# One mixing-and-FFN block of an RWKV-6 layer: the low-rank mix products move from three reduced-precision passes to one float32 product on 32 rows, and the state products move ahead

## The chip, the core and the metric

The kernel runs on one core of a Trainium2 chip. Its engines are TensorE (PE, matrix products; its weight loads are shown apart as PEld), VectorE (DVE), ScalarE (ACT), GpSimd (POOL) and SyncE (SP, which here only issues DMAs). They run side by side and meet at semaphores. The metric is the device time of one launch in microseconds; lower is better.

## The reference

The input x has 4 rows of 1024 tokens with 256 channels. `xn = layernorm(x)`, and the result is x plus two branches of `xn`. Cut to what matters:

```
dxa = shift(xn) - xn;  xm = xn + dxa * miu_x
lora_h = tanh(xm @ A_lora).reshape(b, t, 5, 32)             # five streams of rank 32
miu = lambda_ + einsum('btfi,fic->fbtc', lora_h, B_lora)    # "mix product": [t,32] x [32,256] per stream
w_in, k_in, v_in, r_in, g_in = xn + dxa * miu               # streams W, K, V, R, G
k, v, r = k_in @ Wk.T, v_in @ Wv.T, r_in @ Wr.T;  g = silu(g_in @ Wg.T)
w = td_miu + tanh(w_in @ td_A) @ td_B
y = wkv6(r, k, v, w, u)        # S = diag(exp(-exp(w_t))) S + k_t^T v_t, per head of 64
attn = (groupnorm(y) * g) @ Wo.T
ffn = fp4(silu(fp4(xn) @ fp4(Wgate).T) * (fp4(xn) @ fp4(Wup).T)) @ fp4(Wdown).T   # blocks of 16 quantised
```

## The kernel before

The tokens are worked off in 8 steps of 128 tokens times 4 rows (512 columns, `N`). The 256 channels lie as two halves of 128 partitions. Each step has two parts. `front(step)` makes the shifted input, the LoRA products, the five streams and the projections; beside them it finishes the step before ("tail"): the recurrence, its group norm and output projection, and the FFN units 4 to 7. `levels(step)` runs seven doubling levels of the chunked scan, with FFN units 0 to 3 between them. An FFN "unit" is half of the 704 hidden values of one row: gate and up products on PE (`gate_up`, L313), SiLU on ACT, the product on DVE (`ffn_product`, L875), a block scale (`ffn_scale`, L886: L781 to L787) and rounding (`ffn_round`, L894: L793 to L797) on DVE, the scaling back on POOL (`scale_hidden`, L1148: L1155 and L1158), and per two units the transposes (`hidden_transposes`, L327) and the down product (`down`, L338) on PE. Step 0 has no tail; it quantises the FFN weights there instead (`weight_piece`, L799).

Nothing is planned at run time: each engine has its own instruction list, written out by hand, and works it off in order. A late instruction holds up all behind it on its engine.

The mix products are `mix(f, to)` (L298). The rows of `B_lora` of stream f lie at partitions 32f (stream G at 0) of a tile that is zero elsewhere, so the product contracts 128 rows. For accuracy the tile and the tanh output are each split into a high and a low part in float32r, and three products are summed: 2 halves x 3 = 6 matmuls of 512 columns. The low part of the tanh output costs a copy on ACT (L674) and a subtraction on DVE (`split_hidden`, L861); the weights are split once (ACT L759, DVE L1105). The unsplit weights lie in the buffer `dt`, which POOL clears first (L1255).

Around the change, in `front` with a tail, the orders are:

- PE: recurrence, `down` 0, key transposes (L424), `gate_up` 4, `hidden_transposes` 1, LoRA products (L434), state products (L442), `down` 1, wait for the low part, mix W into pair[0], wait for the state update (L448), mix K into pair[1], `gate_up` 5, decay product (L458), mix V, project K (L464), `hidden_transposes` 2 (it waits for unit 5), decay product 2 (L470), y transposes, `down` 2, `gate_up` 6, mix R, value product (L490), output projection (L394), `gate_up` 7, mix G, project R, transposes, project G.
- DVE: bonus (L949), `shift_mix` (L850), `add_down` 0, `y_stats`, the whole of unit 4, `split_hidden`, the state update (L992, L998), stream W and stream K (L870), `add_down` 1, unit 5, stream V, `head_quant`, and so on.
- POOL: `scale_hidden` 3, `y_centre`, `scale_hidden` 4, add_x W and K (L1146), `y_scale` (L1191), `scale_hidden` 5, add_x V, and so on.

Of the kernel before, what the change touches and what calls it, by code (L numbers as in the profile page):

```python
# [86 lines left out]
def through(step, n=1):  # L87

    return step * n + n


def before(step, n=1):

    return step * n


def later(step):

    return not isinstance(step, int) or step > 0
# [8 lines left out]
def build(nc, x, vecs, w_lora, b_lora, td_a, td_b, w_proj, w_gu, w_dn, ident, masks, head_ones, out):  # L108
    with ExitStack() as ctx:
        def sb(name, shape, dt=F32):  # L110
            return ctx.enter_context(nc.sbuf_tensor(name, shape, dt))
# [7 lines left out]
        walora = sb("walora", [P, HALVES, 2 * P])  # L119
        wblora_hi = sb("wblora_hi", [P, MIXES, C], F32R)  # L120
        wblora_lo = sb("wblora_lo", [P, MIXES, C], F32R)
        wtda = sb("wtda", [P, HALVES, P])
# [23 lines left out]
        xmt = sb("xmt", [P, HALVES, N])  # L146
        lh = xmt
        lh_hi = sb("lh_hi", [P, 2, N], F32R)
        lh_lo = sb("lh_lo", [P, 2, N], F32R)
        xx = sb("xx", [P, MIXES, HALVES, N])  # L150
        tdh = sb("tdh", [P, N])
        ee = sb("ee", [P, HALVES, N])
        dt = sb("dt", [P, 2 * HBS * L])
        wblora = dt[:, 0:MIXES * C].rearrange("p (f c) -> p f c", c=C)
        kk = sb("kk", [P, HBS, L])
# [36 lines left out]
        def sem(name):  # L192
            return ctx.enter_context(nc.semaphore(name))
# [15 lines left out]
        s_bon, s_rup, s_msk, s_y, s_gnvar, s_state = sem("s_bon"), sem("s_rup"), sem("s_msk"), sem("s_y"), sem("s_gnvar"), sem("s_state")  # L209
        s_xql, s_wlo, s_lhi, s_llo, s_bhi, s_blo = sem("s_xql"), sem("s_wlo"), sem("s_lhi"), sem("s_llo"), sem("s_bhi"), sem("s_blo")  # L210
        s_z, s_xqn, s_att, s_hm, s_hqn, s_fo, s_wq = sem("s_z"), sem("s_xqn"), sem("s_att"), sem("s_hm"), sem("s_hqn"), sem("s_fo"), sem("s_wq")
# [22 lines left out]
        def _(sp):  # L234
# [18 lines left out]
            for f in range(4):  # L253
                sp.dma_start(wblora[R_LORA * f:R_LORA * (f + 1), f, :], b_lora[f]).then_inc(s_const, 16)
            sp.dma_start(wblora[0:R_LORA, 4, :], b_lora[4]).then_inc(s_const, 16)
            sp.dma_start(wtda[:, :, 0:TD_R], td_a.rearrange("(h p) c -> p h c", p=P)).then_inc(s_const, 16)
# [18 lines left out]
        def _(pe):  # L275
# [9 lines left out]
            def head_transposes_q(step):  # L285
# [10 lines left out]
                t.then_inc(s_txq, 1)  # L296

            def mix(f, to):  # L298

                for h in range(HALVES):  # L300
                    for n, (ws, ls) in enumerate(((wblora_hi, lh_hi), (wblora_lo, lh_hi), (wblora_hi, lh_lo))):
                        mm = pe.matmul(to[:, h * N:(h + 1) * N], ws[:, f, h * P:(h + 1) * P], ls[:, f // 4, :], start=(n == 0), stop=(n == 2))  # L302
                mm.then_inc(s_miu, 1)

# [110 lines left out]
            def front(step, tail=True):  # L415

                prev = step - 1
                if tail:
                    recurrence(prev)
                    down(prev, 0)  # L420

                    pe.wait_ge(s_xnt, through(step))
                    for hb in range(HBS):
                        t = pe.transpose(pair[1][:, hb * P:(hb + 1) * P], kk[:, hb, :], ident_sb)  # L424
                    t.then_inc(s_tk, 1)
                    gate_up(prev, 4)
                    hidden_transposes(prev, 1)

# [8 lines left out]
                if tail:  # L437

                    pe.wait_ge(s_ktok, through(prev))
                    for hb in range(HBS):  # L440
                        h, b = hb // B, hb % B
                        mm = pe.matmul(pair[1][:, hb * P:(hb + 1) * P].rearrange("p (q j) -> p q j", q=2), ktok[:, hb, :], vv[:, b * HALVES + h], start=True, stop=True)  # L442
                    mm.then_inc(s_kv, 1)
                    down(prev, 1)
                pe.wait_ge(s_llo, through(step))
                mix(W_MIX, pair[0])
                if tail:
                    pe.wait_ge(s_state, through(prev))  # L448
                else:
                    pe.wait_ge(s_xnt, through(step))  # L450
                mix(K_MIX, pair[1])
                if tail:
# [105 lines left out]
            head_transposes(0)  # L558
            pe.wait_ge(s_blo, 1)
            front(0, tail=False)  # L560
# [12 lines left out]
        def _(act):  # L573
# [71 lines left out]
            def both(ap):  # L645
                return ap.rearrange("p (h n) -> p h n", h=HALVES)
# [13 lines left out]
            def front(step, tail=True):  # L660
# [8 lines left out]
                act.wait_ge(s_lora, through(step))  # L669
                act.activation(lh[:], both(pair[0][:]), ACT.Tanh).then_inc(s_lh, 1)  # L670
                act.wait_ge(s_lh, through(step))
                if later(step):
                    act.wait_ge(s_miu, before(step, 5))
                act.copy(lh_hi[:], lh[:]).then_inc(s_lhi, 1)  # L674
                if tail:
# [82 lines left out]
            act.wait_ge(s_const, 16 * CONST_LOADS)  # L758
            act.copy(wblora_hi[:], wblora).then_inc(s_bhi, 1)  # L759
            head_xnt(0)  # L760
# [16 lines left out]
        def _(v):  # L777
# [67 lines left out]
            def shift_mix(step):  # L845
# [8 lines left out]
                ins.then_inc(s_xm, 1)  # L854

            def split_hidden(step):

                v.wait_ge(s_lhi, through(step))
                if later(step):
                    v.wait_ge(s_miu, before(step, 5))  # L860
                v.tensor_tensor(lh_lo[:], lh[:], lh_hi[:].bitcast(F32), ALU.subtract).then_inc(s_llo, 1)  # L861

# [111 lines left out]
            def front(step, tail=True):  # L974
# [3 lines left out]
                if not tail:  # L978
                    weight_piece(0)
                    split_hidden(step)  # L980
                    weight_piece(1)
                if tail:
# [3 lines left out]
                    y_stats(prev)  # L986
                    ffn_unit(prev, 4)
                    split_hidden(step)

# [13 lines left out]
                stream(step, K_MIX, 1, pair[1])  # L1003
                if tail:
                    add_down(prev, 1)
                    ffn_unit(prev, 5)
                else:
                    weight_piece(2)
# [93 lines left out]
            for h in range(HALVES):  # L1102
                v.tensor_scalar(bonus_w[:, h, :], bonus_w[:, h, :], vec[:, U_BONUS + h:U_BONUS + h + 1], None, ALU.mult).then_inc(dve_own, dve_did.one())
            v.wait_ge(s_bhi, 1)
            v.tensor_tensor(wblora_lo[:], wblora, wblora_hi[:].bitcast(F32), ALU.subtract).then_inc(s_blo, 1)  # L1105
            front(0, tail=False)
# [15 lines left out]
        def _(pool):  # L1122
# [70 lines left out]
            def front(step, tail=True):  # L1193
                prev = step - 1
                shift(step)
                if tail:
                    scale_hidden(prev, 3)
                    y_centre(prev)
                    scale_hidden(prev, 4)
                else:  # L1200
                    scale_weights(0)
                    scale_weights(1)
                add_x(step, W_MIX, 0)
                add_x(step, K_MIX, 1)
# [114 lines left out]
```

## Time and profile before

| | |
|---|---|
| median of 3 runs | 894.67 us (892.15 to 896.7) |
| the profiled execution | 890.86 us, span of its instructions 889.1 us |
| PE busy | 770.3 us (87%), 4858 matmul records |
| PE weight loads | 610.5 us (69%) |
| DVE busy | 704.4 us (79%) |
| POOL busy | 458.3 us (52%) |
| ACT busy | 230.9 us (26%) |
| mean granted TensorE clock | 0.937 of full speed |

A busy share is an average over stages. PE's records overlap (one ends while the next has begun), so for PE the distance between the starts of two records is the better measure. A float32 matmul leaves two records, each with its own weight load; a float32r matmul leaves one. The eight fronts start 100 to 107 us apart.

### The profile page before, as it was taken

To read this page: it belongs to the slowest core of one execution; us is meant where nothing else is said; L and a number is where in the kernel's file an instruction comes from. 1 tells how busy PE (TensorE), PEld (TensorE's weight loads), DVE (VectorE), ACT (ScalarE), POOL (GpSimd) and SP (SyncE) were. 2 spreads that over 40 slices of the span, in tenths; PEclk is the share of its full clock that TensorE was granted. 3 is DMA by queue.
4 is the path that set the end of the run, shared out by engine and by line. 5 is a ranking of instruction groups with operands and counts; after the bars stand their busy time and mean duration, and the time that the engine had idled before them with its cause. 6 is when DMAs were issued, how large, how long until landed. Compare 5 with 4: busy or idle time off the path is not lost.

```text
span 889.1 us, 13466 instructions
## 1 busy us (share of the span) xinstructions
PE 770.3 (87%) x4858; PEld 610.5 (69%) x4858; DVE 704.4 (79%) x1245; ACT 230.9 (26%) x341; POOL 458.3 (52%) x321
## 2 busy tenths in 40 slices
PE   0586889988999889998899989998899989998886
PEld 0253876768767777668877678577776678577775
DVE  2898858968898768888689697987888788887774
ACT  2032032421324113330324203241224203241111
POOL 3455546635565346654366344753566445753552
PEclk9897969999999869999799899998999999998999
DMA  6000000000000000000000000000000000000000
GB/s 207 0 1 24 1 1 1 1 24 2 24 1 24 1 24 1 0 24 0 24 0 0 24 0 24 0 24 0 24 0 0 24 0 24 0 1 1 25 1 24
DMA packets 12910, 12.87 MB, mean 14 GB/s; under 512 B 1008, under 2 KB 12624, under 8 KB 12880
## 3 DMA queue, kind: packets, MB, share of 16 engines
q1 hardware_dynamic: 12880, 12.47, 4.3%
q8 instruction: 19, 0.31, 0.1%
q14 instruction: 11, 0.09, 0.0%
HBM read 8.27 MB, written 4.19 MB: 14 GB/s over the span
## 4 chain that ended last, share of the span: by engine, by line
PE 37%; DVE 29%; issue 16%; POOL 13%; ACT 2%; SPq 1%; DMA 1%; POOLq 0%; DVEq 0%
PE pair L364 6%; PE gu L323 6%; PE ft L342 4%; PE pair L394 3%; PE pair L537 3%; POOL raw L1155 3%; DVE dt L1032 3%; POOL kk L1178 3%; PE pair L302 3%; PE pair L490 3%; DVE att L938 3%; POOL xx L1146 2%; DVE hsc L783 2%; DVE hv L797 2%; DVE hv L884 2%
## 5 line engine op out<-in xcount | busy, mean ns | idle before, releaser
L364 PE MATMUL pair<-rr,kk 64*128 64x64 f32 x1792 | 127.5, 294 | 23.9 <-DVE ee L1045 15.2
L364 PEld LDWEIGHTS pair<-rr,kk 64*128 64x128 f32 x1792 | 120.2, 207 | 36.6 <-issue 27.9
L1155 POOL TENSOR_TENSOR raw<-hv,hmg 128x352 f32<-128x352 f32 x64 | 68.3, 1068 | 102.4 <-DVE hv L797 102.4
L1178 POOL TENSOR_TENSOR kk<-kk,dt 128x512 f32<-128x512 f32 x48 | 70.1, 1460 | 97.7 <-PE pair L364 97.7
L634 ACT ACTIVATE sg<-gu 128x352 f32<-128x352 f32 x64 | 29.7, 465 | 334.2 <-PE gu L323 334.2
L323 PE MATMUL gu<-wgu_hi,xqt_hi 128*128 128x352 f32 x256 | 92.5, 361 | 21.9 <-DVE hv L884 21.9
L1146 POOL TENSOR_TENSOR xx<-xx,xnt 128x1024 f32<-128x1024 f32 x40 | 87.1, 2189 | 41.7 <-DVE xx L870 41.7
L342 PE MATMUL ft<-wdn,raw 128*128 128x256 f32 (+1 forms) x384 | 99.1, 401 | 1.0 <-ACT raw L643 0.9
L309 PE MATMUL pair<-xx,wproj 128*128 128x512 f32 x192 | 88.9, 607 | 3.3 <-POOL xx L1146 3.3
L323 PE MATMUL gu<-wgu_hi,xqt_lo 128*128 128x352 f32 x256 | 85.5, 334 | 0.0
L323 PE MATMUL gu<-wgu_lo,xqt_hi 128*128 128x352 f32 x256 | 85.5, 334 | 0.0
L342 PEld LDWEIGHTS ft<-wdn,raw 128*128 128x128 f32 (+1 forms) x384 | 70.2, 196 | 20.5 <-issue 10.9
L323 PEld LDWEIGHTS gu<-wgu_hi,xqt_hi 128*128 128x128 f32 x256 | 50.7, 198 | 29.2 <-DVE hv L884 24.7
L870 DVE SCALAR_TENSOR_TENSOR xx<-pair,vec,dxt 128x512 f32<-128x512 f32 x80 | 56.1, 744 | 17.7 <-PE pair L302 17.5
L309 PEld LDWEIGHTS pair<-xx,wproj 128*128 128x128 f32 x192 | 36.7, 195 | 40.8 <-issue 39.5
L1158 POOL TENSOR_TENSOR raw<-raw,hsc 128x352 f32<-128x352 f32 x64 | 59.3, 926 | 5.0
L787 DVE TENSOR_TENSOR hv<-hv,hsc 128x352 f32<-128x352 f32 x64 | 58.5, 914 | 2.2
L919 DVE TENSOR_TENSOR rr<-rr,dt 128x512 f32<-128x512 f32 x48 | 35.6, 742 | 21.6 <-PE pair L364 21.6
L323 PEld LDWEIGHTS gu<-wgu_lo,xqt_hi 128*128 128x128 f32 x256 | 50.9, 199 | 0.5
L323 PEld LDWEIGHTS gu<-wgu_hi,xqt_lo 128*128 128x128 f32 x256 | 50.5, 197 | 0.0
L938 DVE COPY_PREDICATED att<-masks_sb,pair 128x1024 f32<-128x1024 uint32 x32 | 49.7, 1554 | 0.0
L302 PE MATMUL pair<-lh_hi,wblora_hi 128*128 128x512 f32 x80 | 37.8, 472 | 11.4 <-DVE state L998 6.1
(151 smaller groups left out, 1567.2 us busy)
## 6 DMA issues: line engine op xcount, KB each, us to landing
xl<-in_x SPq DMA_DIRECT2D x8, 512.0 KB, 3.7
out<-raw SPq DMA_DIRECT2D x8, 512.0 KB, 2.8
raw<-in_w_gu SPq DMA_DIRECT2D x1, 1408.0 KB, 9.5
wproj<-in_w_proj SPq DMA_DIRECT2D x1, 1280.0 KB, 6.4
raw<-in_w_dn SPq DMA_DIRECT2D x1, 704.0 KB, 10.3
walora<-in_w_lora SPq DMA_DIRECT2D x1, 160.0 KB, 2.3
dt<-in_b_lora SPq DMA_DIRECT2D x5, 32.0 KB, 1.9
consts<-in_ident SPq DMA_DIRECT2D x1, 64.0 KB, 1.8
```

The source lines that it names most:

```text
L302: mm = pe.matmul(to[:, h * N:(h + 1) * N], ws[:, f, h * P:(h + 1) * P], ls[:, f // 4, :], start=(n == 0), stop=(n == 2))
L309: mm = pe.matmul(to[:, h * N:(h + 1) * N], wproj[:, w, k, h * P:(h + 1) * P], xx[:, f, k, :], start=(k == 0), stop=(k == HALVES - 1))
L323: mm = pe.matmul(gu[:, part * 512:part * 512 + HI], xs[:, k, b * L:(b + 1) * L], ws[:, k, c0:c0 + HI], start=(n == 0), stop=(n == len(term ...
L342: mm = pe.matmul(dn, hxt[0:w, t, :], wdn[0:w, t, :], start=(t == 0), stop=(t == KT - 1))
L364: mm = pe.matmul(to[:, c0:c0 + HS].rearrange("p (n m) -> p n m", m=m), kk[rows, hb, :], odd, start=True, stop=True)
L787: v.tensor_tensor(vbuf.rearrange("p (n k) -> p n k", k=BLOCK), blocks, bcast(sc[:, 1, :], BLOCK), ALU.mult).then_inc(dve_own, dve_did.one())
L870: ins = v.scalar_tensor_tensor(xx[:, f, h, :], src[:, h * N:(h + 1) * N], lam, dxt[:, h, :], ALU.add, ALU.mult)
L938: ins = v.copy_predicated(to[:, :, :, 1, :], bcast(mask, m), data)
L1146: pool.tensor_tensor(x3, x3, xnt0, ALU.add).then_inc(s_xx, 1)
L1155: pool.tensor_tensor(to, hv[:, u % 4, :], hmg[:, u % 2, :], ALU.subtract).then_inc(pool_own, pool_did.one())
L1158: pool.tensor_tensor(to, to, bcast(hsc[:, u % 2, 0, :], BLOCK), ALU.mult).then_inc(s_hx, 1)
L1178: pool.tensor_tensor(k, k, bcast(over, m), ALU.mult).then_inc(s_kup, 1)
```

## The change

The unsplit weights get a tile of their own with two column blocks (streams W, K, V, R in the first, at rows 32f; G in the second), the tanh output a tile of its own, and both splits go. A mix product is now, per half, one float32 matmul that reads 32 rows. Streams W and K are issued alternately, by halves, after both waits. The state products stand right behind `gate_up` 4. On DVE only the product of unit 4 stays ahead of the state update; its scale and rounding move behind streams W and K. On POOL `scale_hidden` 4 moves behind add_x W and K.

```diff
-        wblora_hi = sb("wblora_hi", [P, MIXES, C], F32R)
-        wblora_lo = sb("wblora_lo", [P, MIXES, C], F32R)
+        wblora = sb("wblora", [P, 2, C])
-        lh = xmt
-        lh_hi = sb("lh_hi", [P, 2, N], F32R)
-        lh_lo = sb("lh_lo", [P, 2, N], F32R)
+        lh = sb("lh", [P, 2, N])
-        wblora = dt[:, 0:MIXES * C].rearrange("p (f c) -> p f c", c=C)
...
+            def mix_half(f, to, h):
+                at, t = R_LORA * (f % 4), f // 4
+                return pe.matmul(to[:, h * N:(h + 1) * N], wblora[at:at + R_LORA, t, h * P:(h + 1) * P], lh[at:at + R_LORA, t, :],
+                                 start=True, stop=True)
             def mix(f, to):
-                for h in range(HALVES):
-                    for n, (ws, ls) in enumerate(((wblora_hi, lh_hi), (wblora_lo, lh_hi), (wblora_hi, lh_lo))):
-                        mm = pe.matmul(to[:, h * N:(h + 1) * N], ws[:, f, h * P:(h + 1) * P], ls[:, f // 4, :], start=(n == 0), stop=(n == 2))
-                mm.then_inc(s_miu, 1)
+                mix_half(f, to, 0)
+                mix_half(f, to, 1).then_inc(s_miu, 1)
...
                     gate_up(prev, 4)
+                    pe.wait_ge(s_ktok, through(prev))
+                    for hb in range(HBS):
+                        h, b = hb // B, hb % B
+                        mm = pe.matmul(pair[1][:, hb * P:(hb + 1) * P].rearrange("p (q j) -> p q j", q=2), ktok[:, hb, :], vv[:, b * HALVES + h], start=True, stop=True)
+                    mm.then_inc(s_kv, 1)
                     hidden_transposes(prev, 1)
...
                 if tail:
-
-                    pe.wait_ge(s_ktok, through(prev))
...
-                    mm.then_inc(s_kv, 1)
                     down(prev, 1)
-                pe.wait_ge(s_llo, through(step))
-                mix(W_MIX, pair[0])
+                pe.wait_ge(s_lh, through(step))
                 if tail:
                     pe.wait_ge(s_state, through(prev))
                 else:
                     pe.wait_ge(s_xnt, through(step))
-                mix(K_MIX, pair[1])
+                mix_half(W_MIX, pair[0], 0)
+                mix_half(K_MIX, pair[1], 0)
+                mix_half(W_MIX, pair[0], 1).then_inc(s_miu, 1)
+                mix_half(K_MIX, pair[1], 1).then_inc(s_miu, 1)
...
                 act.wait_ge(s_lora, through(step))
+                if later(step):
+                    act.wait_ge(s_miu, before(step, 5))
                 act.activation(lh[:], both(pair[0][:]), ACT.Tanh).then_inc(s_lh, 1)
-                act.wait_ge(s_lh, through(step))
-                if later(step):
-                    act.wait_ge(s_miu, before(step, 5))
-                act.copy(lh_hi[:], lh[:]).then_inc(s_lhi, 1)
...
-            act.copy(wblora_hi[:], wblora).then_inc(s_bhi, 1)
...
                     weight_piece(0)
-                    split_hidden(step)
                     weight_piece(1)
...
-                    ffn_unit(prev, 4)
-                    split_hidden(step)
+                    ffn_product(prev, 4)
...
                 stream(step, W_MIX, 0, pair[0])
                 stream(step, K_MIX, 1, pair[1])
                 if tail:
+                    ffn_scale(prev, 4)
+                    ffn_round(prev, 4)
                     add_down(prev, 1)
                     ffn_unit(prev, 5)
...
-            v.tensor_tensor(wblora_lo[:], wblora, wblora_hi[:].bitcast(F32), ALU.subtract).then_inc(s_blo, 1)
...
                     y_centre(prev)
-                    scale_hidden(prev, 4)
...
                 add_x(step, K_MIX, 1)
                 if tail:
+                    scale_hidden(prev, 4)
                     y_scale(prev)
                     scale_hidden(prev, 5)
...
-            pool.memset(wblora, 0.0)
```

## Rows read from the trace of the kernel before

**Rows 1.** The page, part 4: the chain that ended last, by engine

```profile
PE 37%; DVE 29%; issue 16%; POOL 13%; ACT 2%; SPq 1%; DMA 1%; POOLq 0%; DVEq 0%
```

**Rows 2.** The chain in order of time (start us, us, what), in the front of step 5

```profile
575.91 0.88 PE ft L335 x6
...
584.29 1.39 PE pair L302 x6
```

**Rows 3.** PE's timeline, same front: start, us, line, operation, [idle before, releaser]

```profile
562.19 0.50 PE L302 MATMUL pair<-lh_hi,wblora_hi 128*128 128x512 f32 x1
...
564.62 0.50 PE L302 MATMUL pair<-lh_hi,wblora_hi 128*128 128x512 f32 x1 [0.77 <-DVE state L998]
...
568.44 1.96 PE L458 MATMUL pair<-xx,wtda 128*128 128x512 f32 x4 [0.23 <-POOL xx L1146]
...
571.63 3.60 PE L309 MATMUL pair<-xx,wproj 128*128 128x512 f32 x8
575.91 0.88 PE L335 MATMUL ft<-consts,raw 128*128 128x128 f32 x6 [0.69 <-POOL raw L1158]
```

**Rows 4.** DVE's timeline, same front

```profile
554.80 0.53 DVE L884 TENSOR_TENSOR hv<-gu,sg 128x352 f32<-128x352 f32 x1
...
556.53 0.52 DVE L787 TENSOR_TENSOR hv<-hv,hsc 128x352 f32<-128x352 f32 x1
...
560.03 1.23 DVE L861 TENSOR_TENSOR lh_lo<-xmt,lh_hi 128x1024 fp32r<-128x1024 f32 x1
...
563.16 1.41 DVE L998 TENSOR_TENSOR state<-pair,state 64x512 f32<-64x512 f32 x2
...
566.33 1.41 DVE L870 SCALAR_TENSOR_TENSOR xx<-pair,vec,dxt 128x512 f32<-128x512 f32 x2 [0.31 <-PE pair L302]
...
568.91 0.52 DVE L884 TENSOR_TENSOR hv<-gu,sg 128x352 f32<-128x352 f32 x1 [0.84 <-ACT sg L634]
...
570.82 1.85 DVE L787 TENSOR_TENSOR hv<-hv,hsc 128x352 f32<-128x352 f32 x1
...
573.90 1.41 DVE L870 SCALAR_TENSOR_TENSOR xx<-pair,vec,dxt 128x512 f32<-128x512 f32 x2
```

**Rows 5.** POOL's timeline, same front

```profile
566.09 4.33 POOL L1146 TENSOR_TENSOR xx<-xx,xnt 128x1024 f32<-128x1024 f32 x2 [2.32 <-DVE xx L870]
570.38 1.91 POOL L1191 TENSOR_TENSOR yy<-yy,gns 128x1024 f32<-128x1024 f32 x1
574.06 0.93 POOL L1155 TENSOR_TENSOR raw<-hv,hmg 128x352 f32<-128x352 f32 x1 [1.78 <-DVE hv L797]
```

**Rows 6.** Timeline of POOL, then of DVE, in step 0

```profile
39.58 4.30 POOL L1146 TENSOR_TENSOR xx<-xx,xnt 128x1024 f32<-128x1024 f32 x2
...
39.87 1.92 DVE L783 TENSOR_SCALAR wsc<-wsc 128x44 f32<-128x44 f32 x1
...
42.29 2.34 DVE L787 TENSOR_TENSOR hv<-raw,wsc 128x704 f32<-128x704 f32 x1
```

**Rows 7.** Timelines of PE and PEld: products that read 64 rows

```profile
532.21 0.33 PE L364 MATMUL pair<-rr,kk 64*128 64x64 f32 x2
...
536.49 0.48 PE L342 MATMUL ft<-wdn,raw 64*128 64x256 f32 x1
...
536.60 0.19 PEld L342 LDWEIGHTS ft<-wdn,raw 64*128 64x128 f32 x1
```

**Rows 8.** PE's timeline in step 0, and a stretch (PE, PEld, DVE, ACT, POOL busy, granted clock)

```profile
41.90 3.75 PE L458 MATMUL pair<-xx,wtda 128*128 128x512 f32 x4 [5.51 <-POOL xx L1146]
...
40.20:47.00 6.80, 5.10 (x8) 2.78 (x9) 6.30 (x6) 0.60 (x1) 3.92 (x3) 0.50 0.00 0
```

**Rows 9.** The chain (first two lines) and DVE's timeline at the start of the launch

```profile
1.27 1.11 POOL dt L1255
...
20.41 1.39 DVE wblora_lo L1105
...
30.73 1.23 DVE L861 TENSOR_TENSOR lh_lo<-xmt,lh_hi 128x1024 fp32r<-128x1024 f32 x1 [3.15 <-ACT lh_hi L674]
```

More of the change, by code:

```diff
@@ L209, in build @@
         s_bon, s_rup, s_msk, s_y, s_gnvar, s_state = sem("s_bon"), sem("s_rup"), sem("s_msk"), sem("s_y"), sem("s_gnvar"), sem("s_state")
-        s_xql, s_wlo, s_lhi, s_llo, s_bhi, s_blo = sem("s_xql"), sem("s_wlo"), sem("s_lhi"), sem("s_llo"), sem("s_bhi"), sem("s_blo")
+        s_xql, s_wlo = sem("s_xql"), sem("s_wlo")
         s_z, s_xqn, s_att, s_hm, s_hqn, s_fo, s_wq = sem("s_z"), sem("s_xqn"), sem("s_att"), sem("s_hm"), sem("s_hqn"), sem("s_fo"), sem("s_wq")
@@ L253, in _ @@
             for f in range(4):
-                sp.dma_start(wblora[R_LORA * f:R_LORA * (f + 1), f, :], b_lora[f]).then_inc(s_const, 16)
-            sp.dma_start(wblora[0:R_LORA, 4, :], b_lora[4]).then_inc(s_const, 16)
+                sp.dma_start(wblora[R_LORA * f:R_LORA * (f + 1), 0, :], b_lora[f]).then_inc(s_const, 16)
+            sp.dma_start(wblora[0:R_LORA, 1, :], b_lora[4]).then_inc(s_const, 16)
             sp.dma_start(wtda[:, :, 0:TD_R], td_a.rearrange("(h p) c -> p h c", p=P)).then_inc(s_const, 16)
@@ L437, in front @@
                 if tail:
-                    pe.wait_ge(s_ktok, through(prev))
-                    for hb in range(HBS):
-                        h, b = hb // B, hb % B
-                        mm = pe.matmul(pair[1][:, hb * P:(hb + 1) * P].rearrange("p (q j) -> p q j", q=2), ktok[:, hb, :], vv[:, b * HALVES + h], start=True, stop=True)
-                    mm.then_inc(s_kv, 1)
                     down(prev, 1)
-                pe.wait_ge(s_llo, through(step))
-                mix(W_MIX, pair[0])
+                pe.wait_ge(s_lh, through(step))
                 if tail:
@@ L558, in _ @@
             head_transposes(0)
-            pe.wait_ge(s_blo, 1)
             front(0, tail=False)
@@ L669, in front @@
                 act.wait_ge(s_lora, through(step))
-                act.activation(lh[:], both(pair[0][:]), ACT.Tanh).then_inc(s_lh, 1)
-                act.wait_ge(s_lh, through(step))
                 if later(step):
                     act.wait_ge(s_miu, before(step, 5))
-                act.copy(lh_hi[:], lh[:]).then_inc(s_lhi, 1)
+                act.activation(lh[:], both(pair[0][:]), ACT.Tanh).then_inc(s_lh, 1)
                 if tail:
@@ L854, in shift_mix @@
                 ins.then_inc(s_xm, 1)
-            def split_hidden(step):
-                v.wait_ge(s_lhi, through(step))
-                if later(step):
-                    v.wait_ge(s_miu, before(step, 5))
-                v.tensor_tensor(lh_lo[:], lh[:], lh_hi[:].bitcast(F32), ALU.subtract).then_inc(s_llo, 1)
             def stream(step, f, n, src):
@@ L1103, in _ @@
                 v.tensor_scalar(bonus_w[:, h, :], bonus_w[:, h, :], vec[:, U_BONUS + h:U_BONUS + h + 1], None, ALU.mult).then_inc(dve_own, dve_did.one())
-            v.wait_ge(s_bhi, 1)
-            v.tensor_tensor(wblora_lo[:], wblora, wblora_hi[:].bitcast(F32), ALU.subtract).then_inc(s_blo, 1)
             front(0, tail=False)
```

## The prediction, made before the changed kernel was run

> **What bounds the kernel now.** I read the page first, its chain of waits above all: PE holds 37% of it, DVE 29%, POOL 13% [rows 1]. So no engine binds alone; the chain hops. Then I read the chain in order of time for one front with a tail (step 5; the front of step 4 has the same lines) and the timelines of PE, DVE and POOL over it. What matters there is one meeting point. PE comes to the hidden transposes of units 4 and 5 (L335) at 575.91, and had idled 0.69 us for POOL [rows 3]; POOL's L1155 for unit 5 had itself waited 1.78 us for DVE's rounding [rows 5]. From 575.91 on the chain stays on PE for the rest of the stream work, the R mix among it [rows 2]. So this front is set by when DVE ends unit 5, and behind it by the sum of PE's work. Ahead of it PE is dense: it reaches the W mix at 562.19 without an idle before it, idles 0.77 for the state update, and waits 0.23 for POOL's add_x W before L458 [rows 3].
>
> **The mix products on PE.** Before, a mix is six float32r records in 1.39 us [rows 2]. A float32 matmul of 512 columns leaves two records: the K projection has 8 of them (four matmuls) in 3.60 us, which is 0.43 each after the 0.17 tail [rows 3]. A lone mix (V, R, G) becomes 2 matmuls = 4 records = 1.72 us, 0.33 more, although it reads 32 rows: the columns set the time. To this I add the switch from 128 rows to few and back. The first W record, behind a 64-row product, takes 0.50 where a record in the run takes its 0.23 pitch plus tail (0.40) [rows 2, 3]; I take 0.15 each way (bounds 0 and 0.3). A lone mix is then dearer by 0.6 (0.33 to 0.9).
>
> W and K lie on rows 0 to 31 and 32 to 63. Do they run side by side? Rows of the level products say so for two groups of 64 rows: two records, 0.32 us each alone, are over in 0.33 together [rows 7]. I take the same for 32: W and K together in 1.72 instead of 2.8 (if not, 3.44).
>
> The Trainium skill ("TensorE: Matmul & The Clock Gate", Part 3, The mechanism) says that a weight load overlaps a running product only when their row groups differ. In a lone mix that would bare three more loads. The trace speaks against it: the second load of a 64-row product begins at 536.60, inside the product that began at 536.49 and lasts 0.48, on the same rows [rows 7]. By the rule's word, with loads of 0.1 bare, R and G would add some 0.6 us a step, 4 us in all; I leave it out of the sum.
>
> **The order in the front, on the clock of step 5.** The state products (16 records) only change places with work of PE's own; PE still reaches W and K at 562.19. DVE no longer does scale and rounding of unit 4 before the state update (from 555.4 to 560.03, 4.6 us) nor the split (1.1) [rows 4]. The state update is ready when unit 4's product is (554.80 + 0.53) and the state products land, about 555.4, and takes 3 us: it ends near 558.5, 3.7 us before PE comes. DVE then stands idle to 562.19 + 0.1 + 1.72 + 0.17 = 564.2. That is the fault of the new order: 5.7 us of DVE's work is taken from a place where it was covered by PE's work, 1.1 of it for good, and 4.6 is put back where PE will wait for it.
>
> - Stream W starts at 564.2 instead of 563.16 + 1.41 = 564.6; four halves of 0.66 end at 566.85 (before: 566.33 + 1.32 = 567.65) [rows 4]. add_x W starts 0.4 sooner, 565.7, and L458 too: 568.05.
> - Scale and rounding of unit 4 follow at 566.85, while POOL runs add_x W and K back to back, 4.33 us [rows 5], to 570.05. In step 0 just this happened: L783 begun inside the first add_x took 1.92 and ended with it, L787 begun inside the second took 2.34 and ended one work time (0.9) after it [rows 6]. So the small scale waits to 567.9, and L787 (0.52 when free [rows 4]) to 570.05; the rounding ends at 571.95. Free it would take 2.9 us and end at 569.8.
> - add_down 1 and unit 5 follow. Before, unit 5 ran from 568.91 to 573.90, 5.0 us, of which L787 lost 1.33 to POOL's L1191 (1.85 against 0.52) [rows 4, 5]. Now it starts at 572.2, and POOL begins scale_hidden 4 at 572.0 (1.8 us) and then L1191 (1.9), to 575.8. L787 can go only at 575.8 and the rounding ends at 577.65, 3.7 us later than before. Free of POOL: 569.8 + 0.35 + 3.6 = 573.75, no delay.
> - POOL's scale_hidden 5 and with it PE's hidden transposes move from 575.91 to 579.6, +3.65 (bounds 0 and 4). Before them PE ends the K projection at 571.63 + 3.6 - 0.4 + 0.6 = 575.4, so it idles about 4.2 us where it idled 0.69.
> - Behind them everything is PE's: R mix and G mix +0.6 each, 1.2.
> - The clock. In step 0 PE idled 5.51 us, and the stretch from 40.20 to 47.00 ran at 0.50 of full speed, 1.2 GHz, before it was back at 2.4 [rows 8]. A wait of 4.2 us is near to that, so I expect a slow stretch in most steps. If half of such a 6.8 us stretch is dense work, 1.7 is lost (bounds 0 and 3.4).
>
> Per tail: 3.65 + 1.2 + 1.7 = 6.55 us. There are 7: 45.9 us (bounds 7 x 0.6 = 4 and 7 x 9 = 63).
>
> **Step 0** gains. The clearing of the buffer goes (1.11, ahead of the loads in the chain), so does the split of the weights (1.39), and DVE no longer stops 3.15 us for the tanh output and splits it (1.14): it can quantise the second weight piece under the LoRA products [rows 9]. Sum 6.8 us on a path that is DVE's to the end of the step. Back go some 1.6 for that piece meeting POOL (L783 and L787 as in rows 6) and 0.7 for the V mix, on which DVE waits: I take -4.5 (bounds -6.8 and -2.5). The last step's finish is untouched. ACT's removed copy (L674) was waited for only through the split, and is counted there.
>
> **Sum.** The profiled execution took 890.86 us (span 889.1, 1.8 around it): 890.9 + 45.9 - 4.5 = 932.3. The median of the runs shown, 894.67, is 3.8 above this execution; I do not add that, it is less than any bound here.
>
> **Rivals.**
> - *No slow clock* after the longer wait: 1.7 x 7 less, 920. For it: PE is dense around the wait. Against: rows 8. Chance 0.12.
> - *W and K do not overlap on PE*, so the change does not do what it says. Both streams then wait: W's last half is done at 562.3 + 6 x 0.43 + 0.17 = 565.05, K's at 565.9; DVE and all behind it +0.9 a step: 938.6. Against: rows 7, though these are 64-row groups. Chance 0.12. With it goes the page's rule on loads, near 937 as worked out from the bare 0.1, chance 0.04.
> - *DVE and POOL slide past each other.* Unit 5 is not late, and each tail pays only the two lone mixes: 7 x 1.2 - 4.5 = +3.9, 894.8. It needs L787 of units 4 and 5 both to miss POOL's operations; the POOL order makes them meet. Chance 0.10.
> - *The other side: step 0 decides.* The place is the first front, where DVE's path is shortened by up to 6.8 us, once. If unit 5 is on time (stream K is done 0.8 us sooner, and free of POOL the units end at 573.75 against 573.98) and the row switches cost nothing, a tail costs 0.33 x 2 - 0.3 = 0.36: 890.9 + 2.5 - 6.8 = 886.6, and a slow stretch of the clock less would take it lower. It decides while a tail costs under 0.64 us (at -4.5) or 0.97 (at -6.8). Against it stands that DVE is idle from 558.5 to 564.2 and its work comes back later. Chance 0.16.
> - The forecast itself: 0.46, with 922 to 942 as its own range.
>
> **Chances and range.** A change of 0.5% (4.5 us) is about what a measurement of this kernel can tell from none. Faster: 0.10 of the last rival, whose time lies at that edge. Within 0.5%: its other 0.06 and half of the one before (0.10), 0.11. Slower: the rest, 0.79. The range runs from 895 to 943: below it lie the last rival and half of the one before, above it the sum of a clock loss of more than 3 us a step and serial W and K.
>
> **What would show it.** Right: in a tail, DVE idle for 5 to 6 us before stream W; L302 records of W and K starting in pairs; L783 and L787 of unit 4 stretched to the ends of POOL's L1146; L335 idle before it 3 to 5 us with POOL's L1158 as releaser, and a clock of 0.5 behind it; each step with a tail 5 to 8 us longer. In step 0 stream W some 5 us sooner. Wrong: L335 waits under 1 us; then the sum is the mixes alone. If the W and K records follow one another at 0.43, the second rival holds.

## The result and the profile after

| | before | changed |
|---|---|---|
| median | 893.41 us (890.82 to 896.7, 4 runs) | 917.68 us (913.55 to 923.18, 4 runs) |
| profiled execution, span | 890.86, 889.1 | 918.57, 916.8 |
| PE / DVE / POOL / ACT busy | 770 / 704 / 458 / 231 | 783 / 694 / 442 / 221 |

The ratio is 1.0273 (95% interval 1.0207 to 1.034): slower by 24 us. Medians in this document take in every run and ratios leave the slow ones out, so a ratio is not always that of two medians. A later comparison of the same kernel (after_again, experiment 7) gave 923.29 (6 runs) against 887.16 (11 runs), ratio 1.0377 (1.031 to 1.0443). DVE, POOL and ACT do less work and the launch is longer, so the time is in waits and on PE. The page says the same: busy time first, then the chain's shares (in [rows 1] PE had 37%, DVE 29%, POOL 13%).

```profile
PE 783.0 (85%) x4778; PEld 586.6 (64%) x4778; DVE 693.9 (76%) x1236; ACT 221.1 (24%) x332; POOL 441.7 (48%) x320
...
PE 48%; DVE 26%; issue 12%; POOL 9%; ACT 2%; SPq 1%; DMA 1%; POOLq 0%; DVEq 0%
```

I cut the launch at two DVE operations: the bonus addition (L949 before, L940 after) and the bonus product (L1045, L1036). From the bonus addition of one step to the bonus product of the next is a front with tail, from there to the next bonus addition a levels part. The stretches of step 5, of the kernel before and then of the changed one (start:end and length in us; busy time of PE, PEld, DVE, ACT, POOL; granted clock; DMA share and GB/s):

```profile
547.99:605.15 57.16, 54.84 (x244) 38.83 (x242) 50.68 (x92) 19.44 (x26) 34.41 (x21) 1.00 0.03 9
605.15:649.35 44.20, 37.95 (x364) 35.06 (x365) 33.94 (x61) 8.89 (x17) 20.27 (x17) 0.92 0.03 12
```

```profile
561.47:624.76 63.29, 57.53 (x234) 36.37 (x232) 49.38 (x90) 18.36 (x25) 31.68 (x21) 0.97 0.03 8
624.76:667.32 42.56, 36.32 (x364) 33.54 (x365) 33.90 (x60) 8.89 (x17) 20.23 (x17) 0.96 0.03 12
```

The front grew by 6.1 us. The seven fronts sum to 401.0 before and 443.9 after, +42.9. Step 0 is 5.6 shorter (its bonus product starts at 78.0 instead of 83.6), the eight levels parts are 10.6 shorter in this execution, and the last part is 1.0 longer: 42.9 - 5.6 - 10.6 + 1.0 = 27.7, the difference of the two profiled executions.

PE's timeline in that front, with the lines that answer to [rows 3]. Take 13.48 off every start to have it on the old clock:

```profile
575.67 1.99 PE L297 MATMUL pair<-lh,wblora 32*128 32x512 f32 x8
...
581.49 1.96 PE L460 MATMUL pair<-xx,wtda 128*128 128x512 f32 x4 [1.71 <-POOL xx L1135]
583.38 1.98 PE L297 MATMUL pair<-lh,wblora 32*128 32x512 f32 x4
585.29 3.70 PE L309 MATMUL pair<-xx,wproj 128*128 128x512 f32 x8
592.62 0.88 PE L335 MATMUL ft<-consts,raw 128*128 128x128 f32 x6 [3.63 <-POOL raw L1147]
593.33 3.45 PE L472 MATMUL pair<-tdh,wtdb 128*128 128x512 f32 x4
```

W and K, 8 records, take 1.99 us; V alone, 4 records, takes 1.98: the two row groups do run side by side. PE comes to W and K at 562.19 on the old clock, to the hundredth where it was. Then L335 waits 3.63 us where it had waited 0.69, and the four records of L472 behind it take 3.45 where four at 2.4 GHz take 1.96 (L460): they ran at 1.2. The stretch at the lower clock is 3.4 us long and full of PE's work; its inner part, in the columns of the stretches above:

```profile
593.60:596.90 3.30, 3.30 (x6) 1.21 (x5) 3.20 (x4) 0.77 (x2) 1.09 (x1) 0.50 0.00 0
```

DVE and then POOL in the same stretch (answers to [rows 4, 5]; L785 here is L787 there, L1135 is L1146, L1180 is L1191):

```profile
570.16 1.41 DVE L987 TENSOR_TENSOR state<-pair,state 64x512 f32<-64x512 f32 x2
577.69 2.73 DVE L861 SCALAR_TENSOR_TENSOR xx<-pair,vec,dxt 128x512 f32<-128x512 f32 x4 [6.12 <-PE pair L297]
...
581.74 2.12 DVE L785 TENSOR_TENSOR hv<-hv,hsc 128x352 f32<-128x352 f32 x1
...
587.52 1.85 DVE L785 TENSOR_TENSOR hv<-hv,hsc 128x352 f32<-128x352 f32 x1
...
590.16 0.53 DVE L795 SCALAR_TENSOR_TENSOR hv<-hv,hmg 128x352 f32<-128x352 f32 x1
```

```profile
579.18 4.29 POOL L1135 TENSOR_TENSOR xx<-xx,xnt 128x1024 f32<-128x1024 f32 x2 [6.08 <-DVE xx L861]
...
587.09 1.90 POOL L1180 TENSOR_TENSOR yy<-yy,gns 128x1024 f32<-128x1024 f32 x1
590.77 0.93 POOL L1144 TENSOR_TENSOR raw<-hv,hmg 128x352 f32<-128x352 f32 x1 [1.78 <-DVE hv L795]
```

The reader is to see a hole and two stretched operations. DVE idles 6.12 us ahead of stream W; then unit 4's L785 is held to the end of add_x K, and unit 5's to the end of y_scale. Unit 5 is rounded at 590.69 and POOL passes it on; only then can L335 start.

### The profile page after: what moved, and what is told of

Its sections match the earlier page's. It is cut to its first block, busy times and chain, and to the rows that moved or that the text cites. A ratio compares the mean times of both kernels' runs of the same rounds, so it can differ in the third digit from the quotient of the medians.

```text
span 916.8 us, 13288 instructions
## 1 busy us (share of the span) xinstructions
PE 783.0 (85%) x4778; PEld 586.6 (64%) x4778; DVE 693.9 (76%) x1236; ACT 221.1 (24%) x332; POOL 441.7 (48%) x320
## 4 chain that ended last, share of the span: by engine, by line
PE 48%; DVE 26%; issue 12%; POOL 9%; ACT 2%; SPq 1%; DMA 1%; POOLq 0%; DVEq 0%
PE ft L342 8%; PE gu L323 7%; PE pair L364 6%; PE pair L297 5%; PE pair L394 3%; POOL kk L1167 3%; PE pair L539 3%; DVE dt L1023 3%; DVE hv L785 3%; PE pair L492 3%; DVE xx L861 3%; PE pair L439 3%; POOL raw L1144 3%; PE pair L472 2%; DVE hsc L781 2%
## 5 line engine op out<-in xcount | busy, mean ns | idle before, releaser
L364 PE MATMUL pair<-rr,kk 64*128 64x64 f32 x1792 | 123.4, 287 | 23.5 <-DVE ee L1036 15.6
L364 PEld LDWEIGHTS pair<-rr,kk 64*128 64x128 f32 x1792 | 116.0, 200 | 36.2 <-issue 28.5
L1135 POOL TENSOR_TENSOR xx<-xx,xnt 128x1024 f32<-128x1024 f32 x40 | 86.9, 2181 | 90.7 <-DVE xx L861 90.7
L1144 POOL TENSOR_TENSOR raw<-hv,hmg 128x352 f32<-128x352 f32 x64 | 63.2, 988 | 110.1 <-DVE hv L795 110.1
L323 PE MATMUL gu<-wgu_hi,xqt_hi 128*128 128x352 f32 x256 | 94.5, 369 | 18.8 <-DVE hv L875 18.7
L635 ACT ACTIVATE sg<-gu 128x352 f32<-128x352 f32 x64 | 29.6, 463 | 316.1 <-PE gu L323 316.1
L342 PE MATMUL ft<-wdn,raw 128*128 128x256 f32 (+1 forms) x384 | 95.3, 390 | 1.0 <-ACT raw L644 0.9
L342 PEld LDWEIGHTS ft<-wdn,raw 128*128 128x128 f32 (+1 forms) x384 | 68.3, 189 | 22.6 <-issue 14.0
L785 DVE TENSOR_TENSOR hv<-hv,hsc 128x352 f32<-128x352 f32 x64 | 70.1, 1096 | 2.2
L297 PE MATMUL pair<-lh,wblora 32*128 32x512 f32 x160 | 63.6, 615 | 2.9 <-ACT lh L673 1.1
L335 PE MATMUL ft<-consts,raw 128*128 128x128 f32 x192 | 30.5, 300 | 30.7 <-POOL raw L1147 30.0
L1147 POOL TENSOR_TENSOR raw<-raw,hsc 128x352 f32<-128x352 f32 x64 | 53.2, 831 | 5.0
```

The source lines that it names most:

```text
L297: return pe.matmul(to[:, h * N:(h + 1) * N], wblora[at:at + R_LORA, t, h * P:(h + 1) * P], lh[at:at + R_LORA, t, :], start=True, stop=True)
L323: mm = pe.matmul(gu[:, part * 512:part * 512 + HI], xs[:, k, b * L:(b + 1) * L], ws[:, k, c0:c0 + HI], start=(n == 0), stop=(n == len(term ...
L342: mm = pe.matmul(dn, hxt[0:w, t, :], wdn[0:w, t, :], start=(t == 0), stop=(t == KT - 1))
L364: mm = pe.matmul(to[:, c0:c0 + HS].rearrange("p (n m) -> p n m", m=m), kk[rows, hb, :], odd, start=True, stop=True)
L785: v.tensor_tensor(vbuf.rearrange("p (n k) -> p n k", k=BLOCK), blocks, bcast(sc[:, 1, :], BLOCK), ALU.mult).then_inc(dve_own, dve_did.one())
L1135: pool.tensor_tensor(x3, x3, xnt0, ALU.add).then_inc(s_xx, 1)
```

## The experiments

"Front" is the stretch above; a kernel's five inner fronts agree within 0.2 us unless the clock fell in one and not in another, so one profile tells them apart well. The launch times scatter by 1 to 2%, on which the last experiments bear. Where an expectation names the launch, compare the front first: the launch also holds the levels, which vary from one execution to the next.

**1. u4_early: the old place of unit 4.**

```diff
-                    ffn_product(prev, 4)
+                    ffn_unit(prev, 4)
...
-                    ffn_scale(prev, 4)
-                    ffn_round(prev, 4)
                     add_down(prev, 1)
...
                     y_centre(prev)
+                    scale_hidden(prev, 4)
...
-                    scale_hidden(prev, 4)
                     y_scale(prev)
```

> The changed kernel with the old place of unit 4's scale and rounding (ahead of the state update on DVE) and of its scaling back on POOL (ahead of add_x W); new mix products, new place of the state products. Order theory: unit 5 is late only because unit 4's rounding stands behind streams W and K. Then a front with a tail (from the bonus L940 to the product for the bonus weights, L1036 of the changed kernel) takes 57.2 (before) + 1.0 (R and G mix) + 0.8 (W waits for the state) = 59.0 us instead of 63.3, L335 waits under 1.5 us, and the launch is near 898. Rival, the float32 mix products themselves cost the time: the front stays above 62 and the launch near 915.

Measured: 878.85 us (4 runs) against 890.24 (7 runs), ratio 0.9872 (0.9782 to 0.9961). The front:

```profile
540.16:598.62 58.46, 55.88 (x234) 35.94 (x232) 49.80 (x90) 18.29 (x25) 33.34 (x21) 1.00 0.03 9
```

58.5 us against the expected 59.0, no clock lost, and PE does not wait at L335:

```profile
568.16 0.87 PE L335 MATMUL ft<-consts,raw 128*128 128x128 f32 x6
```

With the float32 mix products in place, moving unit 4's scale and rounding on DVE and its scaling back on POOL to their old places takes 4.8 us out of an inner front: their order is the cause of that much. The front is left 1.3 us above the old one; the R and G mixes account for 1.2 of it (worked out below, and seen again in experiment 9). The state products stand ahead in this kernel too, so their move is not tested by itself.

The launch was expected near 898 and came in 19 us lower. Step 0 does not explain that. In the two profiled executions the seven fronts are 7.6 us longer than in the kernel before, step 0 is 6.2 us shorter, and the eight levels parts are 13.1 us shorter. The levels put this launch below the old one, and experiment 7 asks whether they belong to the kernel.

**2. u4_fill: unit 4's rounding in DVE's idle time** (ahead of stream W, behind the state update; POOL as in u4_early).

```diff
                     ins.then_inc(s_state, 1)
+                    ffn_scale(prev, 4)
+                    ffn_round(prev, 4)
                 stream(step, W_MIX, 0, pair[0])
...
-                    ffn_scale(prev, 4)
-                    ffn_round(prev, 4)
                     add_down(prev, 1)
```

> The changed kernel with unit 4's scale and rounding put into DVE's 6 us idle time, between state update and stream W, and POOL's scaling back of unit 4 ahead of add_x W again. Order theory: it is covered there by PE's work; unit 5 ends near 2 us sooner than in the kernel before, L335 hardly waits, the front takes 57.2 + 1.0 - 0.5 = 57.7 us, the launch 889 (step 0 keeps its 5.6 us gain). Rival, mix products: front above 62, launch near 915.

Measured: 879.38 us (4 runs), ratio 0.9807 (0.9709 to 0.9905), fronts 57.92 to 58.04, where 57.7 was expected. DVE's rows: the rounding ends at 559.9, and 2.36 us of the hole are left.

```profile
559.39 0.53 DVE L795 SCALAR_TENSOR_TENSOR hv<-hv,hmg 128x352 f32<-128x352 f32 x1
562.27 2.73 DVE L861 SCALAR_TENSOR_TENSOR xx<-pair,vec,dxt 128x512 f32<-128x512 f32 x4 [2.36 <-PE pair L297]
```

So with the state products and streams in the new order the front is only 0.8 us above the old one, less than the 1.2 that the R and G mixes cost: the fault is in what was put behind the streams. In launch time it cannot be told from u4_early, and it too is below its expected 889: its fronts cost 4.8 us in sum, step 0 gives 4.0 back, and the levels are 10.2 us shorter in the profiled execution.

**3. split_new_order: the old mix products in the new order.** The edit is the order part of the change alone, made to the kernel before, with

```diff
                     ins.then_inc(s_state, 1)
+                    split_hidden(step)
                 stream(step, W_MIX, 0, pair[0])
```

> The kernel before (three float32r products per half) with the new order: state products ahead, scale and rounding of unit 4 behind streams W and K, POOL's scaling back of unit 4 behind add_x; the split of the tanh output stands between state update and stream W. Order theory: the front is long here too. PE does W without waiting for the state, so stream W starts near 563.8, K near 565.3; unit 5 is late by 2.8 to 3.3 us and the clock falls: front 61.5 to 62.3 against 57.2. Rival, mix products: front near 57.

Measured: one run, 915.05 us, fronts 62.5 to 63.5. PE's row at L335, then the stretch of step 5's front:

```profile
586.23 1.24 PE L335 MATMUL ft<-consts,raw 128*128 128x128 f32 x6 [4.34 <-POOL raw L1159]
```

```profile
554.46:617.16 62.70, 56.35 (x244) 39.75 (x242) 50.52 (x91) 19.42 (x26) 31.71 (x21) 0.97 0.03 8
```

It is a little over the expected 61.5 to 62.3, and L335 comes 3.85 us later in the front than before, where I had 2.8 to 3.3 for unit 5. Part of that is this kernel's own: the split now stands behind the state update, and PE waits 0.84 us for it ahead of the W mix. With experiment 1 this nearly crosses the two parts of the change: new order with the old products +5.5 a front, new products with unit 4 in its old place +1.3, both +6.1. The two need not add up exactly: there is that wait, and both kernels have the state products ahead.

**4. yscale_late: POOL's y_scale behind scale_hidden 5.**

```diff
                     scale_hidden(prev, 4)
-                    y_scale(prev)
                     scale_hidden(prev, 5)
+                    y_scale(prev)
```

> The changed kernel with POOL's y_scale (1.9 us) behind scale_hidden 5 instead of ahead of it. If unit 5's L785 is held by this POOL operation (1.85 us against 0.52), it now takes under 1 us, L335's wait falls from 3.6 by 1.3 to 1.5, the front from 63.3 to 61.8 and the launch to near 907. Rival, DVE is simply late by its own work: no change, 917.

Measured: 910.99 us (4 runs), ratio 1.0162 (1.0067 to 1.0256). DVE's row of unit 5's L785, PE's row at L335, and the front:

```profile
583.98 0.52 DVE L785 TENSOR_TENSOR hv<-hv,hsc 128x352 f32<-128x352 f32 x1
```

```profile
587.74 0.88 PE L335 MATMUL ft<-consts,raw 128*128 128x128 f32 x6 [2.30 <-POOL raw L1147]
```

```profile
557.93:618.20 60.27, 55.84 (x234) 35.85 (x232) 48.41 (x91) 18.37 (x25) 32.69 (x21) 1.00 0.03 9
```

The operation went from 1.85 to 0.52 and the wait from 3.63 to 2.30, 1.33 each: POOL's operation held it. The same hold of 1.33 stands in the kernel before [rows 4, 5], so it is a gain that can be had and not a part of the 6.1 us. The front gained 3.0, more than expected: with the shorter wait the clock stayed at 2.4 GHz (1.00 in the last row, and in six of the seven fronts), worth the other 1.7. The launch is 4 us above the expected 907 although the fronts are shorter, since the seven later levels parts sum to 319.1 us in its profiled execution against 302.7 in the changed kernel's.

**5. pe_filler: work for PE in the wait.** The results of the extra products are overwritten.

```diff
                 project(pair[0], 0, K_MIX).then_inc(s_kmm, 1)
                 if tail:
+                    for _ in range(4):
+                        pe.matmul(ft[:, 0:N], wtda[:, 0, :], xx[:, K_MIX, 0, :], start=True, stop=True)
                     hidden_transposes(prev, 2)
```

> The changed kernel with 4 extra float32 products of 512 columns (their result is overwritten) on PE ahead of hidden_transposes 2, 3.4 us of work in the 3.6 us wait. Clock theory: the 3.4 us at 1.2 GHz in each front come from that wait; they go, L472 takes 1.9 us instead of 3.45 and the front 63.3 - 1.6 = 61.7 us, the launch near 906. Rival, the clock falls for another reason or PE's extra work only adds: front 63.3 or more, 917 or more.

Measured: 899.83 us (4 runs), ratio 1.0126 (1.0045 to 1.0208). PE's row (L474 here is L472 of the changed kernel) and the front:

```profile
584.03 1.88 PE L474 MATMUL pair<-tdh,wtdb 128*128 128x512 f32 x4
```

```profile
552.17:613.78 61.61, 59.27 (x242) 37.39 (x240) 48.98 (x90) 18.38 (x25) 32.50 (x21) 1.00 0.03 9
```

61.6 against 63.3: the clock's share is 1.7 us a front, as said. Useless work in the wait made the front shorter. The launch is 6 us below the expected 906, with 292.3 us in the seven later levels parts.

**6. wwkk: W's halves first, then K's.**

```diff
                 mix_half(W_MIX, pair[0], 0)
-                mix_half(K_MIX, pair[1], 0)
                 mix_half(W_MIX, pair[0], 1).then_inc(s_miu, 1)
+                mix_half(K_MIX, pair[1], 0)
                 mix_half(K_MIX, pair[1], 1).then_inc(s_miu, 1)
```

> The changed kernel with W's two halves issued first, then K's two (rows 0 to 31 twice, then rows 32 to 63 twice). If PE runs different row groups side by side only when they alternate in the program, the eight records take 3.4 us and the front grows by 0.9 (W and K ready later) to 1.7. If each row group is worked off by itself from a queue, they take 1.9 as before and the front stays at 63.3.

Measured: one run, 915.05 us (by chance the same time as in experiment 3; the traces differ), fronts 63.3 (one of 61.6, where the clock held).

```profile
572.22 1.99 PE L297 MATMUL pair<-lh,wblora 32*128 32x512 f32 x8
```

The same 1.99 us. For these products the alternation buys nothing; the two row groups overlap either way.

**7. before_again and after_again: the two kernels unchanged**, for the part that the forecast had not looked at, the levels.

> The kernel before, unchanged, for a second profile. Fronts 57.2 again. The levels (from the bonus product L1045 to the next bonus L949) are the question: they summed to 365.5 us in the first profile, with 92 us at 1.2 GHz in them. If that sum belongs to the kernel it comes back within 3 us; if it is chance of the execution it differs by 5 us or more.

> The changed kernel, unchanged, for a second profile and more runs. Fronts 63.3 again and step 0 near 78. The levels summed to 354.9 us in its first profile against 365.5 and 367.5 in two of the kernel before, in step with the time at 1.2 GHz. If fewer slow stretches belong to the changed kernel, the sum is again 350 to 358 and the ratio 1.025 to 1.03; if it was chance, the sum can be 365 or more and the ratio goes to 1.04.

Measured: before_again 893.86 us in one run; after_again 923.29 us (6 runs), 926.16 in the profiled one. Fronts: 401.0 in sum, as before, and 442.2 against 443.9, because in one of the seven the clock held (61.6 us). The eight levels parts:

| | before | before_again | changed | after_again |
|---|---|---|---|---|
| levels, us | 365.5 | 367.5 | 354.9 | 363.9 |

So the 10.6 us that the levels gave back came down to 1.6 to 3.6 in the second profile. The launches vary in the same way: in the first profile fronts, step 0 and last part account for 38.3 us, and the two comparisons measured 24.3 and 36.1. So most of the 10.6 did not come back, and whether some of it belongs to the kernel is open. Over all profiles without extra products in the levels, the seven later parts sum to 292.3 to 319.1 us in the seven with float32 mixes throughout, and to 304.7 to 316.1 in the three with the old mixes (before, before_again, split_new_order): the ranges overlap. The length of a levels part goes with its clock: in before_again two parts of the same work are

```profile
402.32:444.91 42.59, 36.34 (x364) 33.56 (x365) 33.92 (x60) 8.89 (x17) 20.28 (x17) 0.96 0.03 12
...
604.15:652.19 48.04, 42.31 (x364) 39.05 (x365) 34.09 (x60) 8.90 (x17) 20.24 (x17) 0.82 0.03 11
```

**8. before_warm and warm: extra products in the short waits of the levels**, in the kernel before and in u4_fill.

```diff
                     pe.wait_ge(s_g, through(step))
+                    pe.matmul(pair[0][:, 0:N], wtda[:, 0, :], xx[:, K_MIX, 0, :], start=True, stop=True)
+                    pe.matmul(pair[0][:, 0:N // 2], wtda[:, 0, :], xx[:, K_MIX, 0, 0:N // 2], start=True, stop=True)
                     pe.wait_ge(s_rk, through(step))
...
+            def idle_work(n):
+                pe.matmul(ft[:, 0:n], wtda[:, 0, :], xx[:, K_MIX, 0, 0:n], start=True, stop=True)
...
                 gate_up(step, 1)
+                if tail:
+                    pe.wait_ge(s_hxt, before(step, 4))
+                    idle_work(N // 2)
                 level(step, 3)
+                if tail:
+                    idle_work(N // 2)
                 gate_up(step, 2)
                 level(step, 4)
+                if tail:
+                    idle_work(N)
+                    idle_work(N // 2)
                 gate_up(step, 3)
```

> The kernel before with the same extra products in the waits of the levels. If the 70 us at 1.2 GHz in its seven later levels parts come from the waits, they fall under 15 and the launch falls by 20 to 28 us, to 865 to 872, with the fronts at 57.2. Rival: no change, 891.

> u4_fill with extra products on PE (results overwritten) in its waits of the levels: ahead of level 0 (1.3 us of work), level 3 (0.4), gate_up 2 (0.4) and gate_up 3 (1.3). Clock theory: the stretches at 1.2 GHz in the levels come from these waits; without them a levels part takes 41 us as where u4_fill had none, the seven later ones lose 20 to 30 us of slow time at half its length, and the launch goes to 865 to 872. Rival, the extra work only delays: levels 42 or more in every step, launch 880 or more.

Measured: before_warm 860.69 us (858.13 to 861.4, 6 runs) against 887.16 (11 runs), ratio 0.9668 (0.9616 to 0.9719); warm 859.08 (856.7 to 860.4), ratio 0.9655 (0.9604 to 0.9707). Steps 2 and 5 of before_warm, and the sum of its seven later levels parts, which was 316.05 before:

```profile
289.62:330.53 40.91, 38.53 (x376) 33.66 (x375) 33.91 (x61) 8.88 (x17) 20.25 (x17) 1.00 0.04 14
...
583.78:624.68 40.90, 38.53 (x376) 33.66 (x375) 33.93 (x61) 8.88 (x17) 20.24 (x17) 1.00 0.04 13
...
sum 283.45, PE 268.15 PEld 234.55 DVE 234.09 ACT 58.88 POOL 139.32; mean PE 38.31 PEld 33.51 DVE 33.44 ACT 8.41 POOL 19.90
```

Useless work of 3.4 us a step (12 more records, 376 against 364) takes 32.6 us out of the levels (28.5 against before_again, whose seven parts sum to 311.9), and the scatter of the launch falls from 12 us (11 runs of the kernel before, same chip) to 3. The expected gain was 20 to 28 us of launch time and it was 26.5; both launches were forecast at 865 to 872 and came in below, from a lower old median. The waits make slow stretches possible and not certain: u4_fill, without the extra products, went through step 5's levels at 2.4 GHz with the same waits that the kernel before has there (1.43, 0.36, 0.71, 0.8 and 1.6 us on PE).

```profile
604.00:644.98 40.98, 34.74 (x364) 32.01 (x365) 33.91 (x60) 8.88 (x17) 20.24 (x17) 1.00 0.04 13
```

**9. hybrid and hybrid_warm: float32 on 32 rows for W and K only.** u4_fill with V, R and G in three float32r products again, the split of the tanh output in DVE's hole, and for the second kernel the extra products of warm.

```diff
-        wblora = sb("wblora", [P, 2, C])
+        wbl_wk = sb("wbl_wk", [P, C])
...
                     ffn_scale(prev, 4)
                     ffn_round(prev, 4)
+                    split_hidden(step)
                 stream(step, W_MIX, 0, pair[0])
...
+                pe.wait_ge(s_llo, through(step))
                 mix(V_MIX, pair[1])
```

> u4_fill, but with float32 on 32 rows for W and K alone; V, R and G mixes are again three float32r products of the split tanh output, whose split (ACT copy, DVE subtraction) stands in DVE's idle time ahead of stream W; the clearing and the split of the weights come back at the start. Theory: R and G cost 0.5 us less each, the split is covered, so the front takes 57.95 - 1.0 = 56.9 us; step 0 is 2 to 3 us longer than in u4_fill; the launch near 875. Rival, the split is not covered (the tanh copy is late or meets POOL): front 58 or more, launch 882 or more.

> hybrid (float32 on 32 rows for W and K alone, unit 4's rounding in the idle time) with the extra products of warm. Both gains are on different stretches, so they add: fronts 56.7, later levels 40.9, step 0 near 81.5: against warm 7 x 1.2 less and 2 more, the launch 851 to 855. Rival, the gains overlap or the split of the weights costs more than 2 us at the start: 858 or more.

Measured: hybrid 881.28 us (8 runs), ratio 0.9882 (0.9837 to 0.9928), with fronts of 56.7, near the expected 56.9: 1.2 us under u4_fill's 57.95, which is the price of the R and G mixes in float32. Its launch is above the expected 875 and not distinct from u4_fill. The profiled execution was the slowest of the eight (890.85 us), so its levels (318.1 us in the seven later parts) say nothing of the kernel. Hybrid_warm, whose clock holds: 851.95 us (849.57 to 855.51, 6 runs) against 888.21 (11 runs), ratio 0.96 (0.9561 to 0.9639), the fastest here. Its front in step 5:

```profile
520.79:577.52 56.73, 53.77 (x241) 37.71 (x240) 50.25 (x92) 19.43 (x26) 33.41 (x21) 1.00 0.03 9
```

## Why the prediction was right, and where its sizes were off

The direction and the mechanism held, in each place that it named. Forecast 932, measured 917.7 and, in the second comparison, 923.3: inside the stated range of 895 to 943, but the first is below the 922 to 942 that the forecast gave itself. Step by step, on the old clock of step 5:

| step | forecast | measured |
|---|---|---|
| PE comes to W and K | 562.19 | 562.19 |
| W and K together | 1.72 + tail 0.17 | 1.99 |
| stream W starts; DVE idle before it | 564.2; 5.7 | 564.21; 6.12 |
| L458 (L460 after) starts | 568.05 | 568.01 |
| unit 5 rounded | 577.65 | 577.21 |
| hidden transposes late by | 3.65 | 3.23 |
| R and G mix, more by | 1.2 | 1.22 |
| clock, a front | 1.7 | 1.7 (experiment 5) |
| an inner tail: the three together | 6.55 | 6.13 |
| seven tails | 45.9 | 42.9 |
| step 0 | -4.5 | -5.6 (after_again: -4.2) |
| levels | 0 | -10.6, then -1.6 |

The lateness is what the rows of DVE and PE gave [rows 3, 4]: work that stood under PE's LoRA products was put behind them, where it meets POOL [rows 5, 6]. It is 3.23 and not 3.65 because DVE began unit 5 at 571.94 on the old clock, where I had 572.2, and ended it in 5.27 us, where I had 5.45; these are sums of pitches that I had rounded up. Ahead of it, unit 4's L785 was held for 1.6 us by add_x K (2.12 against 0.52); what that hold alone is worth was not tested.

The price of a lone mix came out almost to the hundredth. It is read from the start of the product ahead of it to the start of the group behind it, in the R mix before and then after:

```profile
583.96 0.33 PE L323 MATMUL gu<-wgu_hi,xqt_lo 128*128 128x352 f32 x1
584.12 0.39 PE L302 MATMUL pair<-lh_hi,wblora_hi 128*128 128x512 f32 x1
...
585.51 3.61 PE L490 MATMUL pair<-wproj,xx 128*128 128x256 f32 x16
```

```profile
602.36 0.32 PE L323 MATMUL gu<-wgu_hi,xqt_lo 128*128 128x352 f32 x1
602.62 1.98 PE L297 MATMUL pair<-lh,wblora 32*128 32x512 f32 x4
604.53 3.72 PE L492 MATMUL pair<-wproj,xx 128*128 128x256 f32 x16
```

1.55 us became 2.17, 0.62 more. G's mix, read the same way, is 0.60 dearer, 1.22 together. Of 0.62, 0.33 are the columns, and 0.29 are the change between 128 and 32 rows, 0.10 ahead of the mix and 0.19 in it (1.91 less 1.72); I had taken 0.3. And 3.23 + 1.22 + 1.68 is 6.13, the whole growth of the front.

The size of the clock term was right by luck. I had half of a 6.8 us stretch filled with work; in the inner fronts the stretch is 3.4 us long and wholly filled. Both give 1.7. A clock that falls with the wait showed in 19 of the 21 fronts that have the wait of 3.5 to 3.6 us (changed, after_again, wwkk) and in all seven of split_new_order with 4.3; with the 2.2 to 2.3 us of yscale_late it showed in one of seven.

The term that was missing is the levels: the sum set them at no change without a word, and in the first profile they were 10.6 us shorter. That is most of the 13.7 us between the forecast and the first profiled execution; the tails, 3.0 cheaper, are the next term. Experiments 7 and 8 say why it could not be read off one execution: their length goes with how many of the stretches at 1.2 GHz fall into them, and this differs from one execution to the next. What makes it differ is open.

Of the rivals, "no slow clock" fell (L472 at 3.45 us, and experiment 5), "W and K do not overlap" fell (1.99 us for eight records), "DVE and POOL slide past each other" fell (2.12 and 1.85 us). "Step 0 decides" named a true gain, 4.2 to 5.6 us, but it decides in none of these kernels: in experiments 1 and 2 it is smaller than what the fronts add. With "W and K do not overlap" I had coupled a rule that I had set aside (the Trainium skill, "TensorE: Matmul & The Clock Gate", Part 3, The mechanism: a weight load overlaps a product only on another row group). By it a lone mix would have bared its loads; V's four records take 1.98 us, like four records of 128 rows (1.96), so no run here agrees with it for these float32 loads. The same section of the Trainium skill also lets a load that goes to a background weight buffer run ahead, and no run here tells whether that is what happens.

The Trainium skill says in the same section that tiles at different row positions of the array overlap, and this case agrees: 8 records in 1.99 us, whichever way they are ordered.

Expectations behind the prediction missed too. The launches of experiments 1, 2, 4 and 5 were off by 4 to 19 us, of which the levels are the larger part. And in experiment 4 I had the clock fall as before; it did not, with a wait of 2.3 us instead of 3.6, and the front came out 1.5 us under the expected 61.8.

## What to carry to other kernels

When one engine's list is reordered, look at what covers each operation now. Under PE's dense stretch unit 4's 4.6 us of DVE work cost the front next to nothing (u4_early comes to L335 0.08 us later than the kernel before); behind it they made PE 3.2 us late, and the longer wait let the clock fall for another 1.7. Cut the launch at two fixed operations per step and compare the pieces before the sums; here the inner fronts repeated to 0.2 us while the launches scattered by 1%. If one kind of piece varies from step to step with the same work, look at the granted clock there, and try useless products in PE's short waits.

## What the runs showed of the hardware that I had not expected

- The levels, where PE has waits of 0.4 to 1.6 us, hold stretches at 1.2 GHz in every profile here without extra products. With four of the waits filled, the seven later parts had none in before_warm and one in warm. A levels part took 40.9 us at full clock, 42.6 at a mean of 0.96, 48.0 at 0.82 and 50.2 at 0.80, with DVE's busy time at 34 in all of them. Filling the four waits took 3.3% off the launch.
- A float32 product on 32 rows costs what one on 128 rows costs (0.43 us for each of its two records of 512 columns), and two of them on different rows cost that once; going from 128 to 32 rows and back costs 0.29 us more. PE starts the records of both groups together even when the program has two products of one group first.
- L785, a DVE operation with two inputs in SBUF, waited for the running POOL operation to its end, 0.52 becoming 1.85 or 2.12 us, and the wait of 1.33 went when the POOL operation was moved away.
